# Finishing 16 of the 49 node tiles of an attention layer inside its last round, and normalising the tiles in another order

## The chip, the cores and the metric

One program runs on one core of a Trainium2 chip. The metric is the device time of one execution in microseconds (us). Three runs of the kernel before took 4553.86, 4554.82 and 4555.9 us; the median is 4554.82. The engines are named as the profile names them: PE (TensorE, matrix products; PEld is its weight load), DVE (VectorE), ACT (ScalarE), POOL (GpSimd) and SP (SyncE, which issues the plain DMA transfers).

## The reference

Four layers work on `x`, 6250 nodes by 256 numbers; each adds its output to `x` after a layer normalisation of its input. The last two matter here: an attention over 100000 edges, sorted by the node they end in (8 heads of 32 numbers), and a mixture of experts.

```python
# third layer: attention over edges (input: layernorm(x))
scores = einsum('ehd,hd->eh', h_src, attn_src) + einsum('ehd,hd->eh', h_dst, attn_dst)
scores = where(scores > 0, scores, 0.2 * scores)
amax   = maximum(segment_max(scores, dst), 0.0)
w      = exp(scores - amax[dst])
denom  = segment_sum(w, dst) + 1e-12
out    = segment_sum(h_src * (w / denom[dst])[..., None], dst)
x = x + out
# fourth layer: experts (input: layernorm(x)); the choice of 2 of 8 experts
# rests on the mean of all normalised nodes, so it is one choice for all
logits = mean(layernorm(x)) @ Wr + br
...
h = gelu(xf @ W1[e] + b1[e]);  y = h @ W2[e] + b2[e]
x = x + layernorm(sum_e w[e] * y + layernorm(x)) * gamma + beta
```

## The kernel before

**Data.** 128 nodes are a tile; there are NT = 49 tiles, the last with 106 nodes. `xs` holds the residual `x` for all tiles, 256 numbers each, in the SBUF buffer `xs_ring`. During the attention the same buffer is the ring for gathered edge rows, so `xs` is parked in the DRAM tensor `t_xs` and brought back when the ring is no longer used. `acc`, a view of the buffer `big`, holds 264 numbers for each tile: for each of 8 heads 32 sums of weighted messages and, as column HD = 32, the sum of the weights (the denominator).

**Attention.** Edges come in 832 steps of 128, and 16 steps (SBS) are a batch: NSB = 52 batches. POOL gathers the rows of a batch with 16 indirect DMAs into one of three thirds of the ring. Then the engines work on the batch, each through one loop of rounds in which it does a part for batch `k` and the end for batch `p = k - 1`. The end of a batch is, on DVE: `whole_segments` (segment maxima), two `weigh` (rows times their weights, L1867), `rescale` (L1877) and two `add` (L1892), one for each half of 8 steps. PE's `message` (L1730 to L1734) makes the sums of a half in PSUM; `add` puts them into `acc`. The second `message` waits until the first `add` has been done (`s_added`), since both use the same two PSUM banks. Each `message` counts up `s_used`, by which the ring's slots come free.

**Bringing back the residual.** SP does this in three transfers (L1632 to L1634): tiles 17 to 32 after batch 49, tiles 33 to 48 after batch 50, tiles 0 to 16 after batch 51, the last. The block of code ends (a barrier of all engines) when SP has seen all three land and each engine has done its part.

**The next block** finishes the attention and normalises (L1968 to L2082). It works in 7 groups of 7 tiles. DVE first makes the reciprocals of all 49 x 8 denominators (L1991, L1993). Then for each group: `divide` (sums times reciprocals, L1998), POOL adds the residual tile by tile (L1984), DVE's `variance` takes statistics of each tile (L2005) and seven small operations over the group (L2008 to L2017), ACT's `root` the square root (L2039), DVE's `invert` the reciprocal of it and the shift (L2022, L2024). DVE runs `divide` two groups ahead. ACT's `normalise` (L2045) writes a normalised tile to one of four buffers, PE's `turn` (L2069) transposes it into PSUM and `feature_sums` (L2075) adds to the mean over all nodes, ACT's `flat` (L2051) copies the transposed tile out to `tt`, one half of which lies in the free part of `big`. ACT's `root` of the next group stands in its queue after turn 5 of a group's 7 (`n % GT == GT - 2`), so that one `normalise` lies between it and the next group's first. Each engine runs its queue in order.

**After it** a short block chooses the two experts and loads their weights, and a last block with 7 iterations runs them: two matrix products for each expert (L2197, L2205), the weighting, the final normalisation and the output.

The order on each engine is written out by hand in these loops; nothing reorders it.

Of the kernel before, what the change touches and what calls it, by code (L numbers as in the profile page):

```python
# [15 lines left out]
ALU = mybir.AluOpType  # L16
ACT = mybir.ActivationFunctionType
F32 = mybir.dt.float32
# [37 lines left out]
RB = 3  # L56
LINK = P + 1
# [73 lines left out]
def gnn_ffn_kernel(nc, x, src, dst, typ, src_e, dst_first, dst_firsts, g_w1, g_b1, g_w2, g_b2, m_rw, m_w1, m_b1,  # L131
# [10 lines left out]
    with ctx:  # L142
# [696 lines left out]
        with ExitStack() as mo:  # L839
# [692 lines left out]
            with ExitStack() as ph:  # L1532
# [34 lines left out]

                CHAIN = ("score", "fwd", "bwd", "ahead", "behind", "left", "right", "top", "fall", "less")
# [30 lines left out]
                with nc.Block() as b:  # L1599
                    @b.gpsimd  # L1600
                    def _(g):
                        for s in range(STEPS):
# [3 lines left out]
                            if RB <= n < NSB + RB - 2 and j == 8:  # L1606
# [4 lines left out]
                                                 ).then_inc(s_row[slot // 8].sem, 16)  # L1611

                    @b.sync
                    def _(sp):
# [17 lines left out]
                        for n, lo, hi in ((NSB - 3, 17, 33), (NSB - 2, 33, NT), (NSB - 1, 0, 17)):  # L1632
                            sp.wait_ge(s_used.sem, s_used.base + SBS * (n + 1))
                            sp.dma_start(xs_flat[:, lo * D:hi * D], t_xs[:, lo * D:hi * D]).then_inc(s_back.sem, 16)  # L1634
                        sp.wait_ge(s_back.sem, s_back.base + 48)
# [144 lines left out]
                    def _(v):  # L1780
# [119 lines left out]

                        for k in range(-1, NSB + 1):
# [30 lines left out]
                s_added.after(STEPS)  # L1932


        with ExitStack() as ph:
            FC = FF // P
            tt = [sb("f_tt", [P, NPAD], F32, ph), big[:, 0:NPAD]]
# [22 lines left out]
            with ExitStack() as nz, nc.Block() as b:  # L1960
# [6 lines left out]
                def of_group(g):  # L1967
                    return slice(g * GT, (g + 1) * GT)  # L1968
# [10 lines left out]
                def _(g_):  # L1979
                    for g in range(NG):  # L1980
                        g_.wait_ge(s_div.sem, s_div.base + g + 1)
                        for n in range(g * GT, (g + 1) * GT):
# [5 lines left out]
                def _(v):  # L1988
                    c = Tally(v, s_dve)
                    v.memset(square[:], 1.0).then_inc(c.sem, c.up())  # L1990
                    v.tensor_scalar(recip[:], every[:, :, :, HD], 1e-12, None, ALU.add).then_inc(c.sem, c.up())  # L1991
                    v.wait_ge(c.sem, c.value())
                    v.reciprocal(recip[:], recip[:]).then_inc(c.sem, c.up())  # L1993
                    v.wait_ge(c.sem, c.value())

                    def divide(g):
                        num = every[:, of_group(g), :, 0:HD]
                        v.tensor_tensor(num, num, recip[:, of_group(g), :].unsqueeze(3).to_broadcast([P, GT, HEADS, HD]),  # L1998
# [340 lines left out]
```

## Time and profile before

| what | value |
|---|---|
| median of three runs | 4554.82 us |
| profiled execution | 4559.83 us |
| its span in the trace | 4558.0 us |
| PE busy | 2768.8 us, 61% of the span |
| POOL busy | 2594.6 us, 57% |
| DVE busy | 2110.7 us, 46% |
| ACT busy | 1141.0 us, 25% |
| mean granted clock of PE | 0.738 of full speed |

The shares are averages over stages of very different kind, so they say little about a change at one place. The attention's rounds end at about 4070 us of the span, the normalising block runs from 4077 to 4159 us, the choice of the experts to 4180 us, and the experts' block to the end. Times in the rows further down are microseconds from the span's start.

### The profile page before, as it was taken

How to read it: one execution, taken by the hardware profiler on the slowest of the kernel's cores; microseconds unless marked ns; L12 is line 12 of the kernel's file. 1: busy time of each engine (PE TensorE's matmuls, PEld its weight loads, DVE VectorE, ACT ScalarE, POOL GpSimd, SP SyncE). 2: the span in 40 equal slices, each digit the busy share in tenths (PEclk: the TensorE clock that was granted, in tenths of full speed). 3: DMA queues.
4: the chain of work that ended last, by engine and by line, in shares of the span. 5: the costliest groups of instructions: out<-in, count | busy, mean ns of one | idle time of the engine just before them, and what ended most of it. 6: DMA issues, size and time to landing. Idle time of an engine off the chain costs nothing. (4 is left out here: it accounts for less than half of the span.)

```text
span 4558.0 us, 47412 instructions
## 1 busy us (share of the span) xinstructions
PE 2768.8 (61%) x12379; PEld 2184.2 (48%) x12379; DVE 2110.7 (46%) x3857; ACT 1141.0 (25%) x2893; POOL 2594.6 (57%) x2731
## 2 busy tenths in 40 slices
PE   5333433333333333434559899957887877858998
PEld 4333333333333333334447644446666666646665
DVE  7322222224222222224635344458888878864444
ACT  6101111110101111112324322234444444424222
POOL 6677777776777777774520132067777777741000
PEclk9666555665565655556679999978778888876999
DMA  4422222222221221222233355345544444430000
GB/s 130 90 53 53 54 53 53 53 53 72 53 53 53 53 53 53 53 53 96 77 118 107 111 214 194 161 143 140 139 136 140 139 135 140 139 104 22 16 16 24
DMA packets 200821, 409.75 MB, mean 90 GB/s; under 512 B 51763, under 2 KB 125123, under 8 KB 193636
## 3 DMA queue, kind: packets, MB, share of 16 engines
q0 software_dynamic: 102016, 246.46, 20.0%
q1 hardware_dynamic: 84868, 153.14, 9.7%
q10 hardware_dynamic: 13664, 6.91, 0.6%
q8 instruction: 124, 2.03, 0.2%
q14 instruction: 149, 1.22, 0.1%
HBM read 305.56 MB, written 104.44 MB: 90 GB/s over the span
## 5 line engine op out<-in xcount | busy, mean ns | idle before, releaser
L721 POOL DMA_INDIRECT ring<-t_gcn,idx x1564 | 1477.7, 945 | 517.6 <-issue 476.1
L782 PE MATMUL psum<-ring,big 128*128 x3328 | 751.5, 418 | 1232.6 <-SPq L729 1228.6
L782 PEld LDWEIGHTS psum<-ring,big 128*128 128x128 f32 x3328 | 699.9, 321 | 1284.2 <-issue 1284.2
L1609 POOL DMA_INDIRECT xs_ring<-t_msg,idx x832 | 797.2, 958 | 380.3 <-issue 247.1
L807 DVE TENSOR_TENSOR big<-big,psum 128x1024 f32 x208 | 254.0, 1221 | 1449.6 <-PE psum L782 1448.8
L748 ACT COPY psum<-zero_sum 128x1024 f32<-128x1024 f32 x208 | 211.0, 1015 | 1762.4 <-DVE big L807 1744.5
L1734 PE MATMUL psum<-xs_ring,a_hot 128*128 128x264 f32 x1456 | 414.6, 446 | 0.0
L1734 PEld LDWEIGHTS psum<-xs_ring,a_hot 128*128 128x128 f32 x1456 | 335.7, 231 | 76.8
L1498 PE MATMUL psum<-big,a_xnt 128*128 128x512 f32 x784 | 355.0, 596 | 0.5 <-ACT a_xnt L1470 0.5
L1403 POOL DMA_INDIRECT a_back<-t_y,m_addr x98 | 97.9, 999 | 438.6 <-POOLq L1207 279.9
L219 DVE TENSOR_TENSOR big<-dloc,psum 128x1024 f32<-128x1024 f32 x208 | 252.3, 1214 | 4.3 <-PEq L701 4.3
L1867 DVE TENSOR_TENSOR xs_ring<-xs_ring,psum 128x2048 f32<-128x2048 f32 x104 | 236.0, 2270 | 0.9 <-ACT psum L1660 0.9
L1712 PE MATMUL psum<-a_laid,a_hott 128*128 128x64 f32 x1664 | 209.2, 281 | 18.8 <-ACT a_laid L1652 18.8
L1498 PEld LDWEIGHTS psum<-big,a_xnt 128*128 128x128 f32 x784 | 142.6, 192 | 143.2 <-issue 142.3
L1712 PEld LDWEIGHTS psum<-a_laid,a_hott 128*128 128x128 f32 x1664 | 200.2, 197 | 21.4 <-ACT a_laid L1652 19.4
L2205 PE MATMUL psum<-f_w2s,f_hid 128*128 128x256 f32 x784 | 172.9, 381 | 11.2 <-ACT f_hid L2218 11.2
L2205 PEld LDWEIGHTS psum<-f_w2s,f_hid 128*128 128x128 f32 x784 | 148.1, 190 | 40.6 <-issue 21.3
L1438 DVE COPY a_rows<-psum 128x512 f32<-128x512 f32 x98 | 67.8, 691 | 189.5 <-PE psum L1498 189.5
L1756 PE MATMUL psum<-ident,xs_ring 128*128 128x128 f32 x104 | 41.6, 503 | 183.9 <-DMA xs_ring<-t_msg,idx 180.8
L924 POOL DMA_INDIRECT t_tok<-m_xn,m_addr x98 | 99.1, 1012 | 93.6 <-DVE m_addr L1124 65.9
L2241 DVE SCALAR_TENSOR_TENSOR f_ov<-psum,f_wsel,f_ov 128x256 f32<-128x256 f32 x98 | 46.3, 483 | 202.7 <-PE psum L2205 201.8
L1892 DVE TENSOR_TENSOR big<-big,psum 128x264 f32 x208 | 89.2, 429 | 96.1 <-PE psum L1734 63.4
(412 smaller groups left out, 4270.5 us busy)
## 6 DMA issues: line engine op xcount, KB each, us to landing
t_msg<-a_rows SPq DMA_DIRECT2D x49, 1056.0 KB, 3.9
a_near<-t_near SPq DMA_DIRECT2D x52, 512.0 KB, 4.1
ring<-t_gcn,idx POOLq DMA_INDIRECT x1564, 2.5
m_xin<-t_tok SPq DMA_DIRECT2D x105, 128.0 KB, 2.1
t_y<-m_yb SPq DMA_DIRECT2D x105, 128.0 KB, 2.1
xs_ring<-t_msg,idx POOLq DMA_INDIRECT x832
xs_ring<-in_x SPq DMA_DIRECT2D x7, 896.0 KB, 11.5
t_xs<-xs_ring SPq DMA_DIRECT2D x7, 896.0 KB, 6.4
```

Of the source, the lines that this page charges most:

```text
L219: return v.tensor_tensor(buf, dloc[:, bass.ds(start, n)].unsqueeze(2).to_broadcast([P, n, P]), ramp.unsqueeze(1).to_broadcast([P, n, P]), ...
L721: g.indirect_dma_start(out=ring[:, p % HALF_RING * 8 + j, :], out_offset=None, in_=t_gcn[conv], in_offset=bass.IndirectOffsetOnAxis(ap=idx ...
L748: a.copy(sums(q), zero_sum[:, 0:1].unsqueeze(2).to_broadcast([P, GROUP, HID])).then_inc(s_clear.sem, 1)
L782: m = t.matmul(opened[:, bass.ds(to[j], ROW_BYTES)].bitcast(F32), hot[q % 2][:, j, :], ring_bytes[:, bass.ds(at[j], ROW_BYTES)].bitcast(F3 ...
L807: v.tensor_tensor(nodes_at, nodes_at, sums(q), ALU.add).then_inc(s_added.sem, 1)
L924: g_.indirect_dma_start(out=t_tok, out_offset=bass.IndirectOffsetOnAxis(ap=addr[:, k, n:n + 1], axis=0), in_=xn[g % 2][:, j, :], in_offset ...
L1498: m = t.matmul(ps[2 + q][:], xnt[n % 2][:, k * P:(k + 1) * P], wt[:, k, q * 512:(q + 1) * 512], start=(k == 0), stop=(k == KD - 1))
L1609: g.indirect_dma_start(out=ring[:, slot, :, :].rearrange("p h c -> p (h c)"), out_offset=None, in_=t_msg, in_offset=bass.IndirectOffsetOnA ...
L1712: m = t.matmul(ps[2 + h][:, j * 64:(j + 1) * 64], hott[h][:, j, :], laid[h][:, j, :], start=True, stop=True)
L1734: m = t.matmul(two[:, bank, :], *part(j), start=False, stop=j == 7, skip_group_check=True)
L1867: v.tensor_tensor(rows, rows, w.unsqueeze(3).to_broadcast([P, 8, HEADS, HD]), ALU.mult).then_inc(s_scaled.sem, 1)
L2205: m = t.matmul(ps[4 + item % 4][:, 0:D], hid[0][:, k, j * P:(j + 1) * P], w2[e][:, k, :], start=(k == 0), stop=(k == FC - 1))
```

## The change

A constant names 16 tiles, `FINAL = slice(17, 33)`: those whose residual comes back with the first of the three transfers. For them the work of the normalising block, up to the variance, is done at the end of the attention's block.

- DVE, in the round that ends the last batch: `shares()` (reciprocals of 16 x 8 denominators) and `divide(0)` (tiles 17 to 24) stand between `rescale` and the first `add`; `divide(1)` (tiles 25 to 32) and `statistics(0)` between the first and the second `add`; `statistics(1)` and `variance()` behind the loop. `shares` waits for all `add`s of the batches before the last.
- POOL, behind its last gather: a wait for the first transfer's landing, and 16 residual additions in two halves of 8, each behind its `divide`.
- The first transfer counts a semaphore of its own (`s_ld[0]`).
- In the normalising block the groups are the seven ranges 17-32, 0-6, 7-13, 14-16, 33-37, 38-42, 43-48, in this order. The first has only `root` and `invert` left. The reciprocals of the others are made in two pieces. ACT's `root` of a range stands behind `flat` in the turn that lies 5 tiles ahead of the range's first tile (`ROOTS`).
- The half of `tt` that lies in `big` starts at tile 17's place instead of tile 0's.

```diff
+FINAL = slice(17, 33)
@@ attention block, POOL @@
+                        g.wait_ge(s_ld[0].sem, s_ld[0].base + 16)
+                        for h in range(2):
+                            g.wait_ge(s_a.sem, s_a.base + h + 1)
+                            for n in range(FINAL.start + 8 * h, FINAL.start + 8 * h + 8):
+                                x_n = xs[:, n, :].rearrange("p (h d) -> p h d", h=HEADS)
+                                m = g.tensor_tensor(x_n, x_n, acc[:, n, :].rearrange("p (h c) -> p h c", h=HEADS)[:, :, 0:HD], ALU.add)
+                            m.then_inc(s_b.sem, 1)
@@ attention block, SP @@
-                        for n, lo, hi in ((NSB - 3, 17, 33), (NSB - 2, 33, NT), (NSB - 1, 0, 17)):
+                        for n, lo, hi, landed in ((NSB - 3, 17, 33, s_ld[0]), (NSB - 2, 33, NT, s_back), (NSB - 1, 0, 17, s_back)):
...
@@ attention block, DVE @@
+                        def shares():
+                            v.wait_ge(s_added.sem, s_added.base + SBS * (NSB - 1))
+                            v.tensor_scalar(share, node_rows[:, FINAL, :, HD], 1e-12, None, ALU.add).then_inc(c.sem, c.up())
+                            v.wait_ge(c.sem, c.value())
+                            v.reciprocal(share, share).then_inc(c.sem, c.up())
+                            v.wait_ge(c.sem, c.value())
+
+                        def divide(h):
+                            num = node_rows[:, FINAL.start + 8 * h:FINAL.start + 8 * h + 8, :, 0:HD]
+                            v.tensor_tensor(num, num, share[:, 8 * h:8 * h + 8, :].unsqueeze(3).to_broadcast([P, 8, HEADS, HD]),
+                                            ALU.mult).then_inc(s_a.sem, 1)
+
+                        def statistics(h):
+                            v.wait_ge(s_b.sem, s_b.base + h + 1)
+                            for n in range(FINAL.start + 8 * h, FINAL.start + 8 * h + 8):
+                                v.bn_stats(bn6[:, n, :], xs[:, n, :]).then_inc(c.sem, c.up())
+
+                        def variance():
...
                             if p >= 0:
                                 rescale(p)
+                            if p == NSB - 1:
+                                shares()
+                                divide(0)
+                            if p >= 0:
                                 add(2 * p)
+                            if p == NSB - 1:
+                                divide(1)
+                                statistics(0)
...
                                 add(2 * p + 1)
+                        statistics(1)
+                        variance()
...
-            tt = [sb("f_tt", [P, NPAD], F32, ph), big[:, 0:NPAD]]
+            tt = [sb("f_tt", [P, NPAD], F32, ph), big[:, FINAL.start * ROW:FINAL.start * ROW + NPAD]]
@@ normalising block @@
-                def of_group(g):
-                    return slice(g * GT, (g + 1) * GT)
+                RANGES = (FINAL, slice(0, 7), slice(7, 14), slice(14, 17), slice(33, 38), slice(38, 43), slice(43, NT))
+                ORDER = [n for w in RANGES for n in range(w.start, w.stop)]
+                BEGINS = [ORDER.index(w.start) for w in RANGES]
+                range_of = [g for g, w in enumerate(RANGES) for n in range(w.start, w.stop)]
+                ROOTS = {BEGINS[g] - 5: g for g in range(1, len(RANGES))}
...
-                    divide(0)
+                    shares(slice(0, FINAL.start))
+                    invert(0)
                     divide(1)
-                    for g in range(NG):
-                        if g + 2 < NG:
+                    divide(2)
+                    shares(slice(FINAL.stop, NT))
+                    for g in range(1, len(RANGES)):
+                        if g + 2 < len(RANGES):
                             divide(g + 2)
                         variance(g)
                         invert(g)
...
+                        if i in ROOTS:
+                            root(ROOTS[i])
```

DVE's queue at the end of the attention, kernel before. `big` is `acc`, `psum` the sums that `message` left; the 8 pairs of L1899 that stand in each `add` for another case of the data are left out:

```order
L1867 TENSOR_TENSOR xs_ring<-xs_ring,psum 128x64x32 x2
L1870 TENSOR_LOAD nrow
...
L1877 SCALAR_TENSOR_TENSOR big<-psum,big 128x264
...
L1892 TENSOR_TENSOR big<-big,psum 128x264
...
L1892 TENSOR_TENSOR big<-big,psum 128x264
...
L1987 UNCONDITIONAL_BRANCH
L1990 MEMSET f_square 128x128
```

Here `rescale` is followed by the first `add` (two L1892), the second `add` (two more, not shown) and the end of the block. The same place in the changed kernel:

```order
L1918 TENSOR_SCALAR a_prod<-big 128x128
L1920 RECIPROCAL a_prod<-a_prod 128x128
L1925 TENSOR_TENSOR big<-big,a_prod 128x64x32
...
L1903 TENSOR_TENSOR big<-big,psum 128x264
...
L1925 TENSOR_TENSOR big<-big,a_prod 128x64x32
L1931 BN_STATS bn<-xs_ring 128x6 x8
...
L1903 TENSOR_TENSOR big<-big,psum 128x264
...
L1931 BN_STATS bn<-xs_ring 128x6 x8
L1936 TENSOR_TENSOR mean<-bn 128x16
```

Three instructions stand ahead of the first `add` (L1903 now), nine between the two, and fifteen behind the second (eight statistics and seven small operations over 16 columns).

DVE's queue at the start of the normalising block, kernel before:

```order
L1990 MEMSET f_square 128x128
L1991 TENSOR_SCALAR f_recip<-big 128x392
L1993 RECIPROCAL f_recip<-f_recip 128x392
L1998 TENSOR_TENSOR big<-big,f_recip 128x56x32 x3
L2005 BN_STATS bn<-xs_ring 128x6 x7
L2008 TENSOR_TENSOR mean<-bn 128x7
```

And in the changed kernel:

```order
L2054 MEMSET f_square 128x128
L2057 TENSOR_SCALAR f_recip<-big 128x136
L2059 RECIPROCAL f_recip<-f_recip 128x136
L2089 RECIPROCAL rstd<-rstd 128x16
L2091 SCALAR_TENSOR_TENSOR f_shift<-mean,rstd 128x16
L2065 TENSOR_TENSOR big<-big,f_recip 128x56x32 x2
L2057 TENSOR_SCALAR f_recip<-big 128x128
L2059 RECIPROCAL f_recip<-f_recip 128x128
L2065 TENSOR_TENSOR big<-big,f_recip 128x24x32
L2072 BN_STATS bn<-xs_ring 128x6 x7
L2075 TENSOR_TENSOR mean<-bn 128x7
```

The two instructions of `invert` for the first range (L2089, L2091), behind which ACT may normalise, stand behind the reciprocals of 17 tiles; before, they stood behind the reciprocals of 49 tiles, three `divide`s and a whole `variance`.

## Rows read from the trace of the kernel before

**Rows 1.** Chain of work that ended last, in time from 4000: start, length, what.

```profile
4180.07 14.93 PE psum L2197 x32
```

**Rows 2.** Busy time by stretch: us; PE, PEld, DVE, ACT, POOL (count); PEclk, DMA share, GB/s.

```profile
4077.30:4099.00 21.70, 0.00 (x0) 0.00 (x0) 17.27 (x23) 1.49 (x2) 16.26 (x21) 0.50 0.06 13
...
4130.00:4158.00 28.00, 28.00 (x145) 28.00 (x144) 7.48 (x34) 21.41 (x72) 0.00 (x0) 0.50 0.00 1
...
4232.00:4300.00 68.00, 64.58 (x224) 41.82 (x223) 36.94 (x79) 18.81 (x29) 0.00 (x0) 1.00 0.06 19
```

**Rows 3.** Timeline 4010 to 4082: start, length, engine, line, what, [idle before <- releaser].

```profile
4026.70 42.45 SPq L1634 DMA_DIRECT2D xs_ring<-t_xs  x3
...
4031.70 0.95 POOL L1609 DMA_INDIRECT xs_ring<-t_msg,idx  x1 [0.30 <-issue]
...
4057.84 0.43 DVE L1877 SCALAR_TENSOR_TENSOR big<-psum,big 128x264 f32 x1
4063.41 1.00 DVE L1892 TENSOR_TENSOR big<-big,psum 128x264 f32 x2 [5.15 <-PE psum L1734]
...
4065.52 3.28 PE L1734 MATMUL psum<-xs_ring,a_hot 128*128 128x264 f32 x14
4069.03 1.00 DVE L1892 TENSOR_TENSOR big<-big,psum 128x264 f32 x2 [4.62 <-PE psum L1734]
...
4077.37 1.28 ACT L2039 ACT_TABLE_LOAD   x1 [23.66 <-PEq L1599]
```

**Rows 4.** Waits of the DMA queue SP from 4020 to 4080: us, times, longest.

```profile
SPq L1599 <- DMA xs_ring<-t_xs: 7.8, 1, 7.8
```

**Rows 5.** Issues of transfers from 4020 to 4080: count, size, median us to landing.

```profile
xs_ring<-t_xs SPq DMA_DIRECT2D x2, 2048.0 KB, 8.0
xs_ring<-t_xs SPq DMA_DIRECT2D x1, 2176.0 KB, 8.1
```

**Rows 6.** Timeline 4076 to 4120, the first group.

```profile
4077.99 2.60 DVE L1993 RECIPROCAL f_recip<-f_recip 128x392 f32<-128x392 f32 x1
...
4080.63 6.38 DVE L1998 TENSOR_TENSOR big<-big,f_recip 128x1792 f32<-128x1792 f32 x3
4082.74 16.86 POOL L1984 TENSOR_TENSOR xs_ring<-xs_ring,big 128x256 f32<-128x256 f32 x21 [50.10 <-DVE big L1998]
4090.75 2.38 DVE L2005 BATCH_NORM_STATS2 bn<-xs_ring 128x6 f32<-128x256 f32 x7 [3.75 <-POOL xs_ring L1984]
4093.17 0.75 DVE L2008 TENSOR_TENSOR mean<-bn 128x7 f32<-128x7 f32 x1
...
4097.11 0.61 DVE L2017 TENSOR_SCALAR rstd<-rstd 128x7 f32<-128x7 f32 x1
...
4099.02 1.58 ACT L2045 ACTIVATE f_xn<-xs_ring,f_shift,rstd 128x256 f32<-128x256 f32 x3 [1.06 <-DVE f_shift L2024]
...
4099.68 0.69 PE L2069 MATMUL psum<-ident,f_xn 128*128 128x128 f32 x2 [30.88 <-ACT f_xn L2045]
```

**Rows 7.** The same timeline, the second group and what follows.

```profile
4106.61 0.21 ACT L2039 ACTIVATE rstd<-rstd 128x7 f32<-128x7 f32 x1 [2.25 <-DVE rstd L2017]
...
4107.17 2.02 DVE L1998 TENSOR_TENSOR big<-big,f_recip 128x1792 f32<-128x1792 f32 x1
...
4107.36 0.69 PE L2069 MATMUL psum<-ident,f_xn 128*128 128x128 f32 x2 [0.49 <-ACT f_xn L2045]
...
4109.27 4.51 POOL L1984 TENSOR_TENSOR xs_ring<-xs_ring,big 128x256 f32<-128x256 f32 x7 [3.20 <-DVE big L1998]
```

**Rows 8.** Timeline 4120 to 4182: a late group on DVE with POOL done; PE's last tile.

```profile
4132.70 0.17 DVE L2008 TENSOR_TENSOR mean<-bn 128x7 f32<-128x7 f32 x1
...
4133.54 0.17 DVE L2017 TENSOR_SCALAR rstd<-rstd 128x7 f32<-128x7 f32 x1
...
4156.66 0.67 PE L2069 MATMUL psum<-ident,f_xn 128*128 128x128 f32 x2
...
4157.83 0.64 PE L2081 MATMUL psum<-f_shift,f_square 128*128 128x48 f32 x2
```

More of the change, by code:

```diff
@@ L1979, in _ @@
                 def _(g_):
-                    for g in range(NG):
-                        g_.wait_ge(s_div.sem, s_div.base + g + 1)
-                        for n in range(g * GT, (g + 1) * GT):
+                    for g in range(1, len(RANGES)):
+                        g_.wait_ge(s_div.sem, s_div.base + g)
+                        for n in range(RANGES[g].start, RANGES[g].stop):
                             x_n = xs[:, n, :].rearrange("p (h d) -> p h d", h=HEADS)
@@ L1990, in _, with shares @@
                     v.memset(square[:], 1.0).then_inc(c.sem, c.up())
[L1991 to L1994, printed above, removed]
+                    def shares(w):
+                        v.tensor_scalar(recip[:, w, :], every[:, w, :, HD], 1e-12, None, ALU.add).then_inc(c.sem, c.up())
+                        v.wait_ge(c.sem, c.value())
+                        v.reciprocal(recip[:, w, :], recip[:, w, :]).then_inc(c.sem, c.up())
+                        v.wait_ge(c.sem, c.value())
                     def divide(g):
-                        num = every[:, of_group(g), :, 0:HD]
-                        v.tensor_tensor(num, num, recip[:, of_group(g), :].unsqueeze(3).to_broadcast([P, GT, HEADS, HD]),
+                        w = RANGES[g]
+                        num = every[:, w, :, 0:HD]
+                        v.tensor_tensor(num, num, recip[:, w, :].unsqueeze(3).to_broadcast([P, w.stop - w.start, HEADS, HD]),
                                         ALU.mult).then_inc(s_div.sem, 1)
                     def variance(g):
-                        w = of_group(g)
-                        v.wait_ge(s_res.sem, s_res.base + g + 1)
-                        for n in range(g * GT, (g + 1) * GT):
+                        w = RANGES[g]
+                        v.wait_ge(s_res.sem, s_res.base + g)
+                        for n in range(w.start, w.stop):
                             v.bn_stats(bn6[:, n, :], xs[:, n, :]).then_inc(c.sem, c.up())
@@ L2019, in invert @@
                     def invert(g):
[L2020 removed]
+                        w = RANGES[g]
                         v.wait_ge(s_root.sem, s_root.base + g + 1)
@@ L2075, in feature_sums @@
                             t.matmul(ps[6 + k][:, 0:1], xs[0:rows, n, k * P:(k + 1) * P], rstd[0:rows, n:n + 1],
-                                     start=(n == 0), stop=(n == NT - 1))
-                    for n in range(NT):
-                        turn(n)
-                        feature_sums(n)
+                                     start=(i == 0), stop=(i == NT - 1))
+                    for i in range(NT):
+                        turn(i)
+                        feature_sums(i)
                     t.matmul(ps[5][:, 0:NT - 1], square[:], shift[:, 0:NT - 1], start=True, stop=True)
```

68 lines of the change are left out of this document (46 added, 22 removed).

## The prediction

> **What bounds the kernel now.** I read the chain of waits first. Its part from 4180.07 on is PE's, the experts' block [rows 1], and from 4232 to 4300 PE runs there at a granted clock of 1.00 [rows 2]. Nothing of the change is in that block or in the choice of the experts before it, so both move as a whole: the question is when PE finishes the normalising block, whose last tile begins at 4156.66 and ends at 4157.83 [rows 8].
>
> Next the stretches. From 4077.3 to 4099 PE is idle, and DVE (17.27 of 21.70) and POOL (16.26) work; from 4130 to 4158 PE is busy all the time, at a clock of 0.50, the lower level of 1.2 GHz [rows 2]. So the block has a start in which PE waits for the first group, and a rest that PE bounds. The start is in rows 6: reciprocals of 392 columns, three divisions, POOL's first seven additions until 4090.75, statistics, seven small operations until 4097.72, and the first `normalise` at 4099.02. PE starts at 4099.68. From 4107.36 to 4156.66 it turns 42 tiles [rows 7, 8], 1.174 us each, so 49 tiles cost 57.5 us; first tile to end is 58.15, so 0.6 was waiting.
>
> Last, what fills the end of the attention. The last `message` ends near 4068.8, and DVE's second `add` at 4070.03 [rows 3]. Then all compute engines idle, while SP waits 7.8 us for the last transfer of the residual, which takes 8.1 from its issue, to about 4076.9 [rows 4, 5]; the next block begins at 4077.37 [rows 3]. This hole, and DVE's idle times of 5.15 and 4.62 us before its two `add`s [rows 3], are what the change fills. POOL issued its last gather at 4031.70 [rows 3], and the first transfer of the residual was issued at 4026.70 [rows 3] and takes 8.0 us [rows 5], so POOL's new wait for it costs nothing: over 26 us lie between.
>
> **The last round, step by step.** `rescale` ends at 4058.27. `shares` has 128 columns in place of 392: by proportion 0.2 and 0.85 us. `divide(0)` has 2048 columns; 1792 took 2.02 [rows 7], so 2.3. With gaps DVE is done at about 4061.8, while the first `add` could start only at 4063.41 [rows 3]: 1.6 us of cover, cost nothing. `divide(1)` and `statistics(0)` stand before the second `add`. Behind that `add` nobody waits in the attention, since the transfer waits for `s_used`, PE's count; so the `add` may be late.
>
> POOL starts at 4061.85 and needs 7 additions in 4.51 [rows 7], 0.645 each. Its additions and DVE's divisions exclude each other: rows 6 show 7 additions from 4082.74 to about 4090.7, 4.5 us of work plus most of two divisions. So `divide(1)` waits for one addition and runs from 4065.05 to 4067.4, POOL's first half ends at 4069.2, and the second at 4061.85 + 16 x 0.645 + 2.3 = 4074.5. `statistics(0)` (8 x 0.34 by the 2.38 for 7 of rows 6, 2.7 us) is done at 4072.0, the second `add` at 4073.1, `statistics(1)` at 4077.2, `variance`, with POOL idle as in rows 8 (4132.70 to 4133.71, 1.0 us), at 4078.2. The barrier follows a little after the last engine (0.4 us before), so the next block begins at 4078.6 instead of 4077.37: 1.2 us later.
>
> Not shown is a DVE operation with one input in PSUM and one in SBUF beside POOL's additions, which the first `add` now is. Bounds: nothing, as for the statistics, which took 2.38 beside POOL [rows 6]; or two waits of 0.6, as for the small operations with two SBUF inputs (0.75 for what takes 0.17 alone) [rows 6, 8], 1.2 us, which would pass through PE's second `message` to the transfer. A gain is excluded, the work stays. I take nothing: its one SBUF input makes it like the statistics.
>
> The Trainium skill (SBUF — State Buffer, the section on the shared port) says that an operation with at most one SBUF input, outside the two-port modes, does not contend with GpSimd, and that one with two SBUF inputs does. By it the first `add` is free, by the row of small operations it would be 1.2 us late; the statistics' row agrees with the rule.
>
> **The first range.** From the block's begin at 4078.6 ACT loads its table (1.28 [rows 3]) and is ready for `root` at about 4080.0. DVE reaches its reciprocals 0.6 us after the begin [rows 3, 6], a little earlier with fewer columns, and needs 0.9 for 136 columns: 4080.1. Then `invert` over 16 columns, without contention about 0.6 (root begins at 4106.61, the next division behind `invert` at 4107.17 [rows 7]). The first `normalise` starts at about 4080.8, PE at 4081.4, against 4099.68: 18.2 us earlier. Clock: PE is idle from 4068.9 in both kernels, and had 0.50 in the whole start [rows 2]; I keep 0.50 and the pace of 1.174 us.
>
> **What is late next.** Tile 16 of the new order needs range 1. DVE begins its `divide` at 4080.8; POOL starts at 4082.85 and has 4.51 of work plus 2.9 of two divisions in which it is held (7 tiles 2.02, 3 tiles 0.9): 4090.25. Statistics 2.38, to 4092.7; the small operations take 4.55 beside POOL, as in rows 6, since POOL has ten more additions ready: 4097.2. ACT comes to this `root` behind `flat` of tile 9, at about 4081.4 + 9 x 1.174 + 1.4 = 4093.4, and waits 3.8 us. PE has tiles up to 11, done at 4095.5, and gets tile 12 at 4098.1: **2.6 us of waiting**. In the kernel before ACT's wait of 2.25 at the same point left PE idle 0.49 [rows 7].
>
> Ranges 2 and 3 (due near 4104 and 4112) are measured by 4104.2 and 4109.5, in time. Range 4 is not: its `root` is due three tiles after range 3's, near 4115.7, but DVE leaves `invert` of range 3 at 4113.0 and then has a division of 6 tiles (1.75), 5 statistics (1.7) and the small ones beside POOL (2.5): 4119.0. PE gets tile 29 at 4119.8 and was done at 4118.0: **1.8 us**. Ranges 5 and 6 have no addition left in their way and are in time.
>
> Moving half of `tt` costs nothing: same shapes, and it is written only over tiles whose division and addition are over.
>
> **The sum.** PE ends at 4081.4 + 57.5 + 4.4 = 4143.3, against 4157.83: **14.5 us** less. In the profiled execution's own time 4559.83 becomes 4545.3; that execution was 5.0 above the median of 4554.82, which becomes **4540.3**.
>
> **Rivals.**
> - *No waiting.* If the small operations cost 1.0 us rather than 4.55 and 2.5, both waits vanish: 18.9 us less, 4535.9. Against it: rows 6 have them beside POOL, which has additions left here too.
> - *The roots bind.* DVE, ACT and PE hold each other in a ring (`invert` waits for `root`, which waits in ACT's queue behind `flat`, so the next group's division is late). With 0.71 for each small operation, 5.0 us in every range, range 4 comes 2 us later, ranges 2 and 5 cost PE about 1.5 each; with 1.2 for the first `add` and 0.3 at the block's end about 6.5 more waiting: 8.0 us less, 4546.8. For it: three of the ranges are short, 3 or 5 tiles, and the small operations cost the same for 3 as for 7. Against it: with POOL idle they took 1.0 [rows 8], and POOL is done near 4119.
> - *It doesn't take hold*: something other than the first range holds PE at the start, say a barrier waiting for the parameters' loads. PE would start near 4099 still, same time, 4554 to 4556. In rows 6 and 7 every start of PE is released by ACT, and ACT's by DVE.
> - *Slower.* POOL holds the port for its whole batch of additions, not for one. Then the first `add` waits 3.6 us more (to 4067.0, the end of 8 additions begun at 4061.85), PE's second `message` and the transfer with it, and in each of ranges 1 to 4 a small operation waits for a batch of up to 4.5: 3.6 + 18 = 21.6 against 14.5 gained, 7 us slower, 4562. It decides from 14.5 us of such waits. Against it: the longest small operation took 0.75, one addition [rows 6].
>
> **How the numbers follow.** A difference under 0.2%, 9.1 us, can't be told from no change in this kernel. The forecast has 0.72, no waiting 0.09, the roots 0.11, no hold 0.05, slower 0.03. Within 0.2% fall the roots' case mostly and the third: 0.13; slower 0.03; faster 0.84. The range runs from 4534.5, no waiting and 1.4 more for the error of the two starts, to 4548.5, beyond the roots' case.
>
> **What would show it.** The first `add` at 4063.4 still and the last transfer's issue at 4069. The block's begin at 4078.6; a start at 4080 or later means that POOL or the first `add` was slower. The first `normalise` 2.2 us behind the begin. ACT waiting at `root` of ranges 1 and 4 for 3 to 4 us each and PE idle before tiles 12 and 29 and nowhere else; a pace of 1.174 at a clock of 0.50. From the end of this block on, every stretch as long as before. If PE's last tile ends later than 4149, the forecast of the waits is wrong; if PE starts later than 4085, that of the last round.

## The result and the profile after

The changed kernel takes 4545.5 us in the median of 15 runs (4543.70 to 4547.96), against 4555.73 of the kernel before in 15 runs on the same chip (4551.84 to 4557.82). The ratio is 0.9978, 95% interval 0.9971 to 0.9985: 10.2 us faster, 6.8 to 13.2 by the interval. On another chip the same kernel was 11.7 us faster (below, e10). Forecast were 14.5 us and 4540.3; the time is inside the range, and the missing 4 us have a place.

The two profiled executions differ by 16.1 us, more than the change gives. What is told from here on is therefore measured from one fixed event on both sides of which the kernels are comparable: the start of the last round's `rescale`, the last operation on DVE that both have alike. Before, it starts at 4057.84 [rows 3], and after at 4054.88; those 2.96 us lie in unchanged code. From there to the end of PE's last tile (taken as the start of the first matmul on `square`, which stands right behind it and is called PE's last tile from here on) it is 99.99 us before [rows 3, 8] and 87.52 after: 12.5 us. From there to the experts' first matmul it is 22.24 [rows 1, 8] and 22.12, and from that to the end of the span 0.5 us less.

The timeline of the changed kernel from 4050 to 4080 on DVE (start, length, engine, line, what, [idle before <- releaser]), where rows 3 stood before:

```profile
4054.88 0.42 DVE L1888 SCALAR_TENSOR_TENSOR big<-psum,big 128x264 f32 x1
...
4056.50 2.29 DVE L1925 TENSOR_TENSOR big<-big,a_prod 128x2048 f32<-128x2048 f32 x1
4060.38 1.00 DVE L1903 TENSOR_TENSOR big<-big,psum 128x264 f32 x2 [1.58 <-PE psum L1745]
4061.47 2.83 DVE L1925 TENSOR_TENSOR big<-big,a_prod 128x2048 f32<-128x2048 f32 x1
4066.16 2.71 DVE L1931 BATCH_NORM_STATS2 bn<-xs_ring 128x6 f32<-128x256 f32 x8 [1.85 <-POOL xs_ring L1620]
4068.78 0.98 DVE L1903 TENSOR_TENSOR big<-big,psum 128x264 f32 x2
4071.25 2.71 DVE L1931 BATCH_NORM_STATS2 bn<-xs_ring 128x6 f32<-128x256 f32 x8 [1.48 <-POOL xs_ring L1620]
...
4074.92 0.18 DVE L1945 TENSOR_SCALAR rstd<-rstd 128x16 f32<-128x16 f32 x1
4080.77 0.17 DVE L2054 MEMSET f_square<- 128x128 f32 x1 [5.68 <-PEq L1602]
```

The idle 5.15 before the first `add` has shrunk to 1.58, and both lots of statistics are in the round. DVE is done at 4075.10. But the next block's first operation on DVE comes only at 4080.77, after 5.68 us in which nothing computes. The same on POOL and ACT:

```profile
4028.83 0.94 POOL L1612 DMA_INDIRECT xs_ring<-t_msg,idx  x1 [0.30 <-issue]
4058.94 12.27 POOL L1620 TENSOR_TENSOR xs_ring<-xs_ring,big 128x256 f32<-128x256 f32 x16 [29.17 <-DVE big L1925]
...
4080.68 1.28 ACT L2110 ACT_TABLE_LOAD   x1 [29.93 <-PEq L1602]
```

POOL's last addition ends at 4071.21. SP is no longer the last: its waits from 4020 to 4085 (engine, line, what it waited for, total us, times, longest):

```profile
SPq L1646 <- DMA xs_ring<-t_xs: 7.8, 1, 7.8
SPq L1602 <- PEq L1602: 6.4, 1, 6.4
```

It waits for the last transfer as long as before [rows 4], and then 6.4 us more at the block's end. What it waits for is in the view of that line, which lists the sequencers' instructions too (line, queue, operation, count, ns min/median/max, first and last start). First the kernel before, L1599, and then the changed one, L1602:

```profile
L1599 POOLq DRAIN  x1: 24790/24790/24790, 4017.4 to 4017.4; - x1
```

```profile
L1602 POOLq DRAIN  x1: 16069/16069/16069, 4064.4 to 4064.4; - x1
```

Every engine drains at a block's end. POOL's drain ends at 4064.4 + 16.07 = 4080.5 in the changed kernel, 9.3 us behind its last addition, and the next block follows at 4080.68. Before, it ended at 4042.2, 9.5 us behind the last gather (4031.70 + 0.95 [rows 3]): as long, but hidden, because the attention ran on for 35 us. The start of a drain in these rows tells nothing: here it is at 4064.4, with 6.8 us of POOL's additions still to run. Its end does.

The normalising block after, its first range and the two places where ACT and PE wait:

```profile
4082.79 1.58 ACT L2117 ACTIVATE f_xn<-xs_ring,f_shift,rstd 128x256 f32<-128x256 f32 x3 [0.60 <-DVE f_shift L2091]
...
4096.94 0.21 ACT L2110 ACTIVATE rstd<-rstd 128x7 f32<-128x7 f32 x1 [1.77 <-DVE rstd L2084]
```

```profile
4083.45 0.69 PE L2142 MATMUL psum<-ident,f_xn 128*128 128x128 f32 x2 [17.69 <-ACT f_xn L2117]
...
4118.91 0.69 PE L2142 MATMUL psum<-ident,f_xn 128*128 128x128 f32 x2 [1.11 <-ACT f_xn L2117]
...
4142.40 0.64 PE L2155 MATMUL psum<-f_shift,f_square 128*128 128x48 f32 x2
```

PE starts at 4083.45 instead of 4099.68 [rows 6] and idles visibly once, 1.11 us before the 30th tile. By stretch (columns as in rows 2):

```profile
4083.50:4118.00 34.50, 34.30 (x174) 34.12 (x174) 28.07 (x64) 25.27 (x85) 23.74 (x33) 0.50 0.03 6
```

### The profile page after: what moved, and what is told of

Same layout as the page of the kernel before. It is cut to its first block and busy times, and to the rows that moved or that the text cites. A ratio compares the mean times of both kernels' runs of the same rounds, so it can differ in the third digit from the quotient of the medians.

```text
span 4541.9 us, 47421 instructions
## 1 busy us (share of the span) xinstructions
PE 2760.5 (61%) x12379; PEld 2178.5 (48%) x12379; DVE 2106.8 (46%) x3862; ACT 1140.7 (25%) x2893; POOL 2595.1 (57%) x2731
## 5 line engine op out<-in xcount | busy, mean ns | idle before, releaser
L2279 PEld LDWEIGHTS psum<-f_w2s,f_hid 128*128 128x128 f32 x784 | 147.8, 190 | 40.8 <-issue 21.3
L1476 ACT COPY a_rows<-psum 128x512 f32<-128x512 f32 x98 | 57.4, 585 | 291.7 <-PE psum L1499 291.7
```

The lines of the kernel that those rows point to most:

```text
L2279: m = t.matmul(ps[4 + item % 4][:, 0:D], hid[0][:, k, j * P:(j + 1) * P], w2[e][:, k, :], start=(k == 0), stop=(k == FC - 1))
```

## The experiments

All distances are from the start of the last `rescale`. The kernels e1 to e4 ran on a chip on which the kernel before takes 5207.76 us, the others on chips on which it takes 4556 to 4558. Ratios are to the kernel before on the same chip. The changed kernel itself ran only where the result above was taken and beside e8 and e9 (as e10), so what e1 to e7 gain or lose against it is read from the distances. What was measured, in one table:

| kernel | ratio (95%) | first `add` | next block begins | PE's last tile | PE idle within |
|---|---|---|---|---|---|
| before | 1 | 5.6 | 19.5 | 100.0 | 0.6 |
| changed | 0.9978 (0.9971 to 0.9985) | 5.5 | 25.8 | 87.5 | 1.4 |
| e10, changed again | 0.9974 (0.9965 to 0.9983) | 5.5 | 25.9 | 87.6 | 1.4 |
| e1, drain early | 0.997 (0.996 to 0.9981) | 4.3 | 20.7 | 83.7 | 2.7 |
| e2, residual on DVE | 0.9975 (0.9965 to 0.9986) | 4.7 | 20.8 | 82.5 | 1.4 |
| e3, late operation on POOL | one run | 4.5 | 27.8 | 108.3 | |
| e4, the same, drained early | one run | 4.5 | 18.9 | 99.4 | |
| e5, order alone | 1.0007 (0.9998 to 1.0016) | 4.1 | 18.1 | 103.1 | 5.8 |
| e6, split first range | 0.9966 (0.9954 to 0.9978) | 4.3 | 19.9 | 84.3 | 6.0 |
| e7, variance ahead | one run | 4.3 | 20.7 | 82.4 | 1.4 |
| e8, split, mended | 0.9959 (0.9945 to 0.9972) | 5.5 | 18.3 | 81.7 | 5.0 |
| e9, root two ahead | 0.9957 (0.9943 to 0.997) | 5.5 | 20.7 | 81.0 | 0.0 |

The begin is ACT's table load, in e6 and e8 DVE's first operation. PE idle is the distance of its first tile from its last, less 57.53 (49 x 1.174).

The distance from `rescale` isn't rigid. The first `add` starts 4.1 to 4.7 us behind it in e1 to e7 and 5.5 to 5.6 in the others, since PE's first `message` of that round is shorter in them: its last 14 matmuls take 4.39 to 4.94 us and not 5.75 to 5.84, at a mean granted clock of 0.65 (e3), 0.66 (e1) and 0.69 (e5) over the `message`, against 0.55 (before, changed) and 0.56 (e9, e10). Where SP's last transfer ends the round (before, e3 to e5) the begin moves with it. Where POOL's additions and DVE behind them end it, it doesn't: 20.7 in e1, e7 and e9 alike.

**e1, a drain behind the last gather.** One line, on POOL in the attention, with all else as changed:

```
                                                 ).then_inc(s_row[slot // 8].sem, 16)
+                        g.drain()
                         g.wait_ge(s_ld[0].sem, s_ld[0].base + 16)
```

> The changed kernel with one more instruction: POOL empties its queue (a drain) right behind its last gather, 26 us before its new additions. Theory A (the drain at the end of a block on POOL costs 9.3 us once whenever POOL has issued indirect DMAs since the last drain, and the change moved this cost from a place where POOL was idle to behind the additions): the drain at the block's end shrinks to under 0.5 us, the next block begins 0.4 to 0.6 us after DVE's last small operation, that is 20.7 us after the last rescale instead of 25.8, and the kernel is 5 us faster than the changed one, near 4540.5. Rival B (9.3 us is what the end of this block costs behind any last POOL operation): begin at 25.8 after the rescale still, 4545.5, no change. Rival C (the early drain delays the wait for the transfer or the additions): the first addition starts later than 4.1 us after the rescale, time between or above.

Measured, the drain's own line, the block's end and the begin behind it:

```profile
L1615 POOLq DRAIN  x1: 16069/16069/16069, 4665.9 to 4665.9; - x1
```

```profile
L1602 POOLq DRAIN  x1: 7687/7687/7687, 4715.4 to 4715.4; - x1
```

```profile
4706.65 0.43 DVE L1889 SCALAR_TENSOR_TENSOR big<-psum,big 128x264 f32 x1
...
4727.36 1.28 ACT L2111 ACT_TABLE_LOAD   x1 [24.83 <-PEq L1602]
```

The early drain ends at 4682.0, 9.2 us behind the last gather (4671.78 + 0.95), and nobody waits for it. The last one ends at 4723.1, 0.1 us behind the last addition. The block begins 20.7 us behind `rescale` instead of 25.8. This is the begin that was forecast (4078.6 - 57.84 = 20.8), and DVE is what ends the round. The kernel is 15.4 us faster than before (9.9 to 20.8 by the interval, which holds the changed kernel's gain too), and PE's last tile comes 3.8 us earlier than in the changed kernel: 5.1 earlier at the start, 1.3 given back to waiting, which now shows before the 13th tile.

**e2, the residual on DVE.** The 16 additions are two operations on DVE, and POOL does nothing behind its gathers:

```
+                        def residual(h):
+                            at = slice(FINAL.start + 8 * h, FINAL.start + 8 * h + 8)
+                            ...
+                            v.tensor_tensor(x_n, x_n, node_rows[:, at, :, 0:HD], ALU.add).then_inc(s_b.sem, 1)
```

> The changed kernel with the 16 residual additions of the attention block on DVE (two operations of 2048 columns, 2.3 us each) and none on POOL; divide(1) stands behind the second add. Theories A and B both: POOL's last work is its last gather, its drain is over 30 us before the end, DVE ends about 21.2 us after the last rescale (adds, 2.3 + 2.7 between them, then 2.3 + 2.3 + 2.7 + 1.1), the next block begins at 21.6 instead of 25.8: 4.2 us faster than the changed kernel, near 4541.3. If the block begins at 25 or later all the same, the late begin is not POOL's.

```profile
4707.19 0.43 DVE L1881 SCALAR_TENSOR_TENSOR big<-psum,big 128x264 f32 x1
...
4713.04 2.29 DVE L1926 TENSOR_TENSOR xs_ring<-xs_ring,big 128x2048 f32<-128x2048 f32 x1 [0.17 <-issue]
...
4727.94 1.28 ACT L2112 ACT_TABLE_LOAD   x1 [24.87 <-PEq L1602]
```

The begin is at 20.8 here too, 0.8 earlier than I had put it. So the 5.1 us go whether the late additions are taken from POOL or its drain is done before them. Eight additions cost 2.29 us on DVE and some 6 on POOL; with POOL's work gone DVE loses nothing, since it had waited for POOL.

**e3 and e4, the drain in the kernel before.** In the kernel before, one memset of 256 columns on POOL, behind the wait for all three transfers; e4 has the drain behind the last gather too:

```
+                        g.drain()          (e4 alone)
+                        g.wait_ge(s_back.sem, s_back.base + 48)
+                        g.memset(late[:], 1.0)
```

> The kernel before the change with one more POOL operation at the end of the attention block: a memset of 256 columns (output not used) that waits until all three transfers of the residual have landed, 19.2 us after the last rescale. Theory A: behind it the drain takes 9.3 us, the next block begins near 29.2 us after the rescale instead of 19.5, and the time is 9.7 us longer. Rival (the late begin in the changed kernel is due to POOL's additions contending with DVE or the transfer): the begin moves by the memset alone, under 1 us.

> As e3_late_pool_op, with a drain on POOL right behind its last gather. Theory A: the first drain takes the 9.3 us where POOL is idle anyway and the second costs nothing, so the next block begins about 20.1 us after the last rescale, within 1 us of the kernel before. Rival B (any last POOL operation costs 9.3 us at this block's end): 29.2 as in e3_late_pool_op.

The timeline and the drain of e3:

```profile
4703.77 0.43 DVE L1880 SCALAR_TENSOR_TENSOR big<-psum,big 128x264 f32 x1
...
4721.84 0.31 POOL L1614 MEMSET a_late<- 128x256 f32 x1 [52.29 <-DMA xs_ring<-t_xs]
...
4731.60 1.28 ACT L2042 ACT_TABLE_LOAD   x1 [31.96 <-PEq L1600]
```

```profile
L1600 POOLq DRAIN  x1: 9529/9529/9529, 4721.8 to 4721.8; - x1
```

And of e4:

```profile
4709.57 0.43 DVE L1881 SCALAR_TENSOR_TENSOR big<-psum,big 128x264 f32 x1
...
4728.42 1.28 ACT L2043 ACT_TABLE_LOAD   x1 [22.98 <-PEq L1600]
```

```profile
L1600 POOLq DRAIN  x1: 391/391/391, 4727.8 to 4727.8; - x1
```

A memset of 0.31 us makes the kernel before wait 9.5 us in its drain, and 0.39 with an earlier drain. That refutes that any last operation on POOL has this tail: it takes something that POOL has left undrained, here since a last gather 52 us earlier. Both kernels begin the next block a little over 1 us earlier than was expected, 1.1 of it because the first `add` does; the difference between them, 9.0, is the theory's.

That what is left undrained is the gathers rests on where else the tail stands. The kernel before has it at the end of an earlier block too, where a memset follows 98 gathers:

```profile
2847.60 7.48 POOL L1405 MEMSET big<- 128x8840 f32 x1
```

```profile
L1395 POOLq DRAIN  x1: 17562/17562/17562, 2845.6 to 2845.6; - x1
```

The drain ends at 2863.2, 8.1 us behind the memset. Each block of that kernel in which POOL issues indirect transfers ends so, 5.9 to 9.5 us behind its last operation. In the blocks without them the drain ends within 0.1 us of POOL's work (L1960), or lasts 0.03 to 0.05 us where POOL has none. No run varied the gathers by themselves.

**e5, the order alone.** The new order of tiles with none of the work in the attention:

```
-RANGES = (FINAL, slice(0, 7), slice(7, 14), ...
+RANGES = (slice(25, 33), slice(17, 25), slice(0, 7), slice(7, 14), ...
```

> The changed kernel with nothing of the final tiles done in the attention: its last round is as in the kernel before, and all 49 tiles are divided, summed and measured in the normalising block, in nearly the new order (tiles 25 to 32, 17 to 24, 0 to 6, 7 to 13, 14 to 16, 33 to 37, 38 to 42, 43 to 48). Theory (the gain comes from work put into the attention's last round, not from the order): the block begins about 19.5 us behind the last rescale as before; PE starts some 18.5 to 20 us behind its begin instead of 22.3, since a first range of 8 tiles has only two divisions of 8 tiles ahead of its measuring, and then waits about 1 us: the end of the transposes 96 to 99 us behind the rescale against 100.0 before and 87.5 in the changed kernel, 1 to 4 us faster than before. Rival (the new order and its ranges are what gains): 90 us or less, 10 us faster than before.

```profile
4060.93 0.43 DVE L1881 SCALAR_TENSOR_TENSOR big<-psum,big 128x264 f32 x1
...
4079.03 1.28 ACT L2092 ACT_TABLE_LOAD   x1 [22.23 <-PEq L1602]
...
4091.78 2.71 DVE L2054 BATCH_NORM_STATS2 bn<-xs_ring 128x6 f32<-128x256 f32 x8 [3.11 <-POOL xs_ring L2030]
...
4109.15 0.21 ACT L2092 ACTIVATE rstd<-rstd 128x8 f32<-128x8 f32 x1 [6.10 <-DVE rstd L2066]
```

```profile
4100.71 0.69 PE L2124 MATMUL psum<-ident,f_xn 128*128 128x128 f32 x2 [30.28 <-ACT f_xn L2099]
...
4109.90 0.69 PE L2124 MATMUL psum<-ident,f_xn 128*128 128x128 f32 x2 [4.33 <-ACT f_xn L2099]
```

The rival is refuted: the order gains nothing. My own size was wrong too. PE's last tile is at 103.1 us and not at 96 to 99; the time is 3.8 us above the kernel before, which the interval can't tell from none. From the begin, which is 1.4 earlier here for the earlier `add`, to PE's last tile it is 85.0 against 80.5 before. Two things were missed. The first range is hardly quicker with 8 tiles: PE starts 21.7 us behind the begin (22.3 before). Its statistics wait 3.11 us for POOL's first eight additions, which take 9.0 us (4082.77 to 4091.78) beside two whole divisions (4.49), the second lot of reciprocals and a third division (2.02), where eight by themselves would take 5.2 (8 x 0.645). And ACT, in its fixed order, asks for range 1's root five tiles ahead of it, at the 4th tile, stands there 6.1 us and lets PE idle 4.33 us, though the tiles 5 to 8 were ready.

**e6, the first range split.** On top of e1: only 8 of the 16 tiles are measured in the attention, their root on ACT and the reciprocal of it on DVE there too; SP no longer waits for the last transfers, POOL does in the next block. The other ranges are 25-32, 0-5, 6-12, 13-16, 33-37, 38-42 and 43-48, and range 5's variance stands ahead of range 4's inversion:

```
-                        sp.wait_ge(s_back.sem, s_back.base + 32)
...
                                 statistics(0)
+                                variance(FIRST)
...
-                        statistics(1)
-                        variance()
+                        invert()
...
+                    g_.wait_ge(s_back.sem, s_back.base + 32)
```

> The version that the traces point to: the drain behind the last gather; only tiles 17 to 24 are measured and inverted in the attention (8 tiles, their root on ACT too, so the table load falls there), tiles 25 to 32 are divided and summed there and measured in the block; the last two node transfers are waited for by POOL in the block, no longer by SP at the attention's end; one range's variance ahead of the inversion that waits. Theory: what ends the attention is then POOL's last addition, about 16.5 us behind the last rescale; the block begins at about 17 us (20.7 with the drain alone), its first normalise within 0.7 us, PE's last transpose 75 to 78.5 us behind the rescale (83.7 with the drain alone, 87.5 changed, 100.0 before); 21 to 25 us faster than before, ratio about 0.9955. Rival (the attention's end is held by something else, DVE's round trip to ACT or the barrier itself): the block begins at 19 us or later and the end is at 80 us or more.

The rival won. DVE after e6's `rescale`, and the place where PE waits:

```profile
4063.97 0.42 DVE L1892 SCALAR_TENSOR_TENSOR big<-psum,big 128x264 f32 x1
...
4075.25 2.71 DVE L1935 BATCH_NORM_STATS2 bn<-xs_ring 128x6 f32<-128x256 f32 x8 [3.11 <-POOL xs_ring L1623]
...
4080.64 0.17 DVE L1949 TENSOR_SCALAR rstd<-rstd 128x8 f32<-128x8 f32 x1
4082.18 1.00 DVE L1907 TENSOR_TENSOR big<-big,psum 128x264 f32 x2 [1.38 <-issue]
```

```profile
4104.80 0.69 PE L2157 MATMUL psum<-ident,f_xn 128*128 128x128 f32 x2 [5.80 <-ACT f_xn L2133]
```

The variance stands ahead of the second `add`, whose sums PE had ready at 4073.67 and which starts at 4082.18 (1.38 us of that are idle with no wait that the profile shows). The small operations run beside POOL's additions, four of them at 0.43 to 0.71. That put the begin at 19.9 and not at 17. And the shorter first range makes a later one late by more than was won: PE idles 5.80 us before the 13th tile, again where ACT stands at a root five tiles ahead.

**e7, one variance ahead.** On top of e1, DVE measures range 4 before it inverts range 3:

```
                         if g == 3:
+                            variance(4)
                         invert(g)
```

> The kernel with the drain behind the last gather and one edit on DVE: the statistics and the variance of range 4 (tiles 33 to 37) stand ahead of the inversion of range 3, which waits 2.9 us for ACT's root. Theory (that wait is what makes ACT wait for range 4's root and PE idle 1.1 us before the 30th tile): ACT's wait there falls from about 2.9 us to under 0.5, PE's idle there vanishes, and PE's last transpose starts 82.3 to 82.9 us behind the last rescale instead of 83.7. Rival (DVE is simply too late with its operations beside POOL's additions): PE still idles 0.8 us or more before that tile.

As forecast: `rescale` at 4056.51, PE's last tile at 4138.93, 82.4 us; the idle before the 30th tile is gone, and one remains, before the 13th:

```profile
4079.99 0.69 PE L2146 MATMUL psum<-ident,f_xn 128*128 128x128 f32 x2 [13.81 <-ACT f_xn L2121]
...
4095.49 0.69 PE L2146 MATMUL psum<-ident,f_xn 128*128 128x128 f32 x2 [1.26 <-ACT f_xn L2121]
...
4138.93 0.64 PE L2159 MATMUL psum<-f_shift,f_square 128*128 128x48 f32 x2
```

**e8, the split mended.** e6 with the variance behind the second `add`, and range 2's root (tiles 0 to 5) two tiles ahead of it:

```
-                                variance(FIRST)
...
+                        variance(FIRST)
                         invert()
...
-                ROOTS = {BEGINS[g] - 5: g for ...
+                ROOTS = {BEGINS[g] - (2 if g == 2 else 5): g for ...
```

> The split version with its two faults mended: the eight tiles' variance stands behind the second add of the last round instead of ahead of it, and ACT takes the root of tiles 0 to 5 two tiles ahead instead of five. Theory: the block begins about 18.5 us behind the last rescale (19.9 in the first split version), PE's first transpose at about 19.5 and its last at 77 to 79 us (84.3 in the first split version, 87.5 in the changed kernel, 100.0 before), with under 2 us of waiting: some 21 us faster than before, ratio about 0.9955. Rival (an earlier begin is eaten again by later ranges that aren't measured in time): PE's last transpose at 81.5 us or later.

The begin and the first transpose are where they were expected (18.3 and 19.1), and the end is not (81.7): the rival's case.

```profile
4077.65 0.69 PE L2157 MATMUL psum<-ident,f_xn 128*128 128x128 f32 x2 [8.26 <-ACT f_xn L2133]
...
4097.70 0.69 PE L2157 MATMUL psum<-ident,f_xn 128*128 128x128 f32 x2 [2.29 <-ACT f_xn L2133]
...
4103.79 0.69 PE L2157 MATMUL psum<-ident,f_xn 128*128 128x128 f32 x2 [2.42 <-ACT f_xn L2133]
...
4140.18 0.64 PE L2170 MATMUL psum<-f_shift,f_square 128*128 128x48 f32 x2
```

PE starts 4.4 us earlier than in e9 and idles 5 us more. By these rows the chain of DVE and POOL for the tiles outside the attention now bounds: tiles 0 to 5 are ready 20.8 us behind the begin (4097.58), while the sixteen tiles ahead of them feed PE for 18.8 us, to 4096.4. The idle of 2.29 shows one tile earlier, before the 16th, since ACT stands at the root ahead of that tile's `normalise`; with the root later still, PE would idle some 1.9 (an estimate: 4097.58 and the 0.7 from an inversion's end to PE, less 4096.4). Then the next range is late again, by 2.42. No run took this chain out, so that it is the bound is argued from the rows.

**e9, the root two ahead.** e7 with range 1's root two tiles ahead of it:

```
-                ROOTS = {BEGINS[g] - 5: g for ...
+                ROOTS = {BEGINS[g] - (2 if g == 1 else 5): g for ...
```

> The drain behind the last gather, range 4's variance ahead of range 3's inversion, and as the one new edit ACT's root of range 1 two tiles ahead of it instead of five. Theory (the wait before the 13th tile is ACT held at a root five tiles early, not a late range): PE's idle of 1.26 us there vanishes and nothing takes its place; the last transpose 81.0 to 81.5 us behind the last rescale against 82.4; about 17 us faster than before, ratio 0.996 to 0.9965. Rival (DVE's range 1 is really too late): the same idle or more appears before the 17th tile.

```profile
4054.38 0.43 DVE L1889 SCALAR_TENSOR_TENSOR big<-psum,big 128x264 f32 x1
...
4075.12 1.28 ACT L2114 ACT_TABLE_LOAD   x1 [24.87 <-PEq L1602]
```

```profile
4077.89 0.69 PE L2146 MATMUL psum<-ident,f_xn 128*128 128x128 f32 x2 [12.65 <-ACT f_xn L2121]
...
4135.41 0.64 PE L2159 MATMUL psum<-f_shift,f_square 128*128 128x48 f32 x2
```

PE's last tile is at 81.03 us (81.0 to 81.5 expected), with no idle between first and last: 57.52 us for 49 tiles, the 1.174 each that the kernel before had. The time is 4536.53 us (5 runs, 4535.31 to 4539.57). On the same chip the kernel before takes 4557.78 and the changed one 4546.10 (10 runs, 4542.87 to 4549.03): it beats both, by 21.3 and 9.6 us (17 expected against before; 13.7 to 26 by the interval). PE's idle before the 13th tile is gone although range 1's small operations took 4.2 us here, no less than in e7 (4.0): it was ACT's place in its order, and not a late range.

**e10, the changed kernel again.**

> The changed kernel once more, unaltered, so that the versions above stand beside it on one chip and its two distances can be seen twice: the block's begin 25.8 and PE's last transpose 87.5 us behind the last rescale, both within 0.3 us if the distances belong to the program (theory), off by a microsecond or more if they vary from run to run (rival); 9 to 12.5 us faster than before.

Begin 25.87, last tile 87.60, 0.1 us from the first profile: with the first `add` at the same place, the distances belong to the program, though `rescale` itself lay anywhere from 4054.4 to 4064.0 in the profiles of those chips on which the kernel before takes 4556 to 4558. 11.7 us faster than before.

## Why the prediction was right, and where it wasn't

**The mechanism was right**: the work was put into a hole, PE started earlier, and nothing behind the block changed. e5 shows that the order has no share in it.

**The step that failed is the end of the last round.** The prediction said "The barrier follows a little after the last engine (0.4 us before), so the next block begins at 4078.6 instead of 4077.37: 1.2 us later." It was 6.3 later. The engine that ends last was right: DVE ends 20.2 us behind `rescale` (78.2 - 57.84 = 20.4 forecast), and SP's transfer comes before it. What was left out is POOL's drain, 9.3 us from its last operation once gathers have been issued. The row from which the 0.4 us came had no POOL work behind the gathers, so the drain had 35 us of cover. The prediction looked at what the new additions wait for, and not at what waits behind them at the block's end. With the drain ahead of them (e1) the begin is where it was forecast. The prediction's own sign misread it as well: a begin at 4080 or later was to mean that POOL or the first `add` was slower. On its axis the begin was at 4083.6, and neither was.

**The first range**: 2.11 us from the begin to the first `normalise` (2.2 forecast), and PE at 0.66 behind it.

**The waits were mis-sized**: 4.4 us forecast, 1.4 measured. Before tile 12 (the 13th, as the prediction counts from 0) there was about 0.2 and not 2.6. Range 1's small operations took 2.7 us from first to last (4094.21 to 4096.90) and not 4.55, since only four of the seven were slowed by POOL's additions (0.53 to 0.68); the other three took 0.15 to 0.17. In e10 and e2 it was 2.7 again. In e1, with the same instructions, they took 4.0 us and PE idled 1.30 there. So what a short operation costs beside POOL isn't fixed, and one row of before was taken for all; that it depends on the phase against POOL's additions is likely, but no run varied the phase alone. The second wait was 1.11 for 1.8, at the tile named (29, the 30th). e7 and e9 show both waits to be what was said, ACT in fixed order at a root, and DVE behind it: with two edits of order they vanish.

**The sum by its own steps**: 14.5, less 5.1 for the begin, plus 3.0 for the waits, is 12.4; measured from `rescale` it is 12.5. The two errors have opposite signs, and that the time came as near as it did is partly luck: with the waits as forecast, the late begin would have left 9.4. The median's 10.2 and 11.7 have intervals that hold it (6.8 to 13.2 and 8 to 16).

**The first `add` beside POOL's additions** was taken as free, with a bound of 1.2 us. It took 1.00 for two, as before [rows 3], 5.50 us behind `rescale` (5.57 before). This agrees with the rule of the Trainium skill (SBUF — State Buffer, "Who interferes with whom"): with at most one SBUF input and outside the two-port modes, an operation doesn't contend with GpSimd. The number of SBUF inputs alone doesn't decide, though: range 1's two `TENSOR_SCALAR`, with one SBUF input each, took 0.54 and 0.60 beside POOL where they take 0.17 with POOL idle, and L2017's 0.61 in rows 6 had shown it.

**The rivals.** No waiting (18.9): refuted, but e9 reaches it, at 19.0. The roots bind: refuted in its sizes; e5 and e8 show the mechanism in other orders, 5 to 6 us of it. It doesn't take hold: refuted, PE starts at 4083.45 and not near 4099. Slower, with POOL holding the port for its whole batch: refuted, DVE's `divide(1)` took 2.83 beside the additions (2.29 in e10) for 2.29 alone, and POOL's 16 additions 12.27, while 16 x 0.645 is 10.3. The clock was 0.50 from begin to end, as forecast.

## What to carry to other kernels

Before work is put on an engine's queue at the end of a block, read the drain of that engine at the block's end, and not only its last operation: a tail that was hidden becomes the path as soon as the engine has something late to do. Where GpSimd has issued gathers and has work behind them, drain it while nobody waits. When a pipeline is fed in ranges, an engine with a fixed order should ask for the next range's result as late as its round trip allows: five tiles early cost 1.3 us in e7 and 4.3 in e5, where the range before had 8 tiles; two tiles early cost nothing in e9. How late is late enough hangs on the other chain: in e8 two tiles early still held one tile that was ready.

## What the runs showed of the hardware that was not expected

- GpSimd's drain after gathers: its end lay 9.5 us behind the last gather (before), 9.2 (e1), and 9.3 and 9.2 us behind the last operation where work came later (the changed kernel; e3, whose drain lasted 9.53 from the memset). After an earlier drain it was 0.1 us (e1) and 0.39 (e4). So it is neither a wait for the gathers' data, which PE had used up by then (its last `message` ends at 4065.8 in the changed kernel), nor a cost of any last operation; it is paid once, at the drain.
- It doesn't grow in step with the number of transfers. In the profile of the kernel before it was 5.9 us behind 70 indirect transfers (the block at L259), 8.1 behind 98 (L1395), 8.8 behind 106 (L891), 9.1 twice behind 782 (L701) and 9.5 behind 832. These blocks differ in more than the number. At the end of L891's, where the indirect transfers come last, nothing hides it: POOL's drain ends at 2319.8, and the next latest, SP's, starts at 2312.8.
- The normalising block, in which GpSimd issues no gather, has no such tail: L2021's drain in the changed kernel ends at 4118.0, where POOL's work ends.
- Eight residual additions cost DVE 2.29 us as one operation over 2048 columns, and GpSimd about 6 us as eight beside DVE's work.
- PE's granted clock was at 0.50, the lower level of 1.2 GHz, while PE was busy nearly all the time with transposes and one-column matmuls (34.30 of 34.50 us in the changed kernel), in the normalising block of each kernel here.
